# A graph attention layer on one core: loads of 2 MB with four held, the next group's lists earlier in a step, packings last and two tiles ahead

## What is computed

```python
h = relu(layernorm(x))
support = h @ weight                  # 4 heads of 64
f1, f2 = support . weight_u, support . weight_v
scores = leaky_relu(f1[m] + f2[n], 0.2) * adj[n, m]
attn   = softmax of scores over the m where scores != 0
out    = attn @ support + bias + h @ proj_w.T + proj_b
return x + out
```

## Time and profile before

| | |
|---|---|
| median of three runs | 863.06 us (859.76 to 864.25) |
| profiled execution | 860.12 us, of which the span 858.4 us |
| PE / DVE / POOL / ACT busy | 83% / 75% / 62% / 15% of the span |
| granted TensorE clock, mean | 0.889 of full speed |
| DMA | 63855 packets, 329.82 MB, mean 384 GB/s |
| DMA queues, share of 16 engines | q1 (SP) 83.8%, q0 (GpSimd's gathers) 11.1%, q10 (ScalarE's stores) 2.4% |
| loads of `adj` | 256 of 1 MB, 13.3 us from issue to landing (median) |
| gathers | 384, 6.2 us from issue to landing (median) |

### The profile page before, as it was taken

How to read it: one execution, slowest core, us unless ns; L and a number is a source line. 1 busy time by engine, 2 the same in 40 slices (tenths; PEclk the granted TensorE clock), 3 DMA queues, 4 the chain that set the end, 5 groups by cost and what they waited for, 6 DMA issues and landing times.

```text
span 858.4 us, 11157 instructions
## 1 busy us (share of the span) xinstructions
PE 710.9 (83%) x3011; PEld 434.2 (51%) x3011; DVE 643.1 (75%) x2740; ACT 129.3 (15%) x467; POOL 529.0 (62%) x598
## 2 busy tenths in 40 slices
PE   2989999999956878887888888788888878888865
PEld 0656666666513545454555445354544445454454
DVE  4556666657446988879869798977979787886887
ACT  0223333333210111000001011000011100000010
POOL 4344455454467776667766667676766766676570
PEclk9999999999966989888879898887989888988789
DMA  9999999999999999999999999999999999999971
GB/s 307 422 407 393 416 422 416 407 423 413 419 410 384 385 401 402 388 405 384 402 393 374 399 374 405 383 404 384 390 396 375 406 366 400 359 403 401 397 302 53
DMA packets 63855, 329.82 MB, mean 384 GB/s; under 512 B 12795, under 2 KB 15560, under 8 KB 31024
## 3 DMA queue, kind: packets, MB, share of 16 engines
q1 hardware_dynamic: 43056, 286.28, 83.8%
q0 software_dynamic: 18432, 34.30, 11.1%
q10 hardware_dynamic: 2304, 8.52, 2.4%
HBM read 328.99 MB, written 16.91 MB: 403 GB/s over the span
## 4 chain that ended last, share of the span: by engine, by line
PE 42%; DMA 25%; DVE 24%; issue 4%; POOL 3%; ACT 1%; POOLq 0%; ACTq 0%; SPq 0%
DMA adj_raw<-in_adj 21%; PE ps_words L400 11%; PE ps_agg L461 9%; PE ps_agg L381 7%; PE ps_two L381 6%; DVE att L933 5%; PE ps_two L400 5%; DVE cand L787 3%; DVE base L943 3%; POOL att L717 2%; DMA att<-support_table,idx 2%; PE ps_score L445 2%; DMA att<-in_x 1%; PE ps_words L392 1%; DMA support_table<-att 1%
## 5 line engine op out<-in xcount | busy, mean ns | idle before, releaser
L717 POOL DMA_INDIRECT att<-support_table,idx x384 | 417.4, 1087 | 188.7 <-issue 105.8
L400 PE MATMUL ps_words<-adj_raw,pack_w 128*128 128x512 fp8e4 x640 | 186.7, 428 | 25.4 <-DMA adj_raw<-in_adj 25.3
L461 PE MATMUL ps_agg<-att,ident 128*128 128x260 f32 x640 | 176.3, 428 | 8.5 <-DVE att L933 8.5
L461 PEld LDWEIGHTS ps_agg<-att,ident 128*128 128x128 f32 x640 | 135.1, 218 | 41.6 <-issue 18.6
L400 PE MATMUL ps_two<-adj_raw,pack_w 128*128 128x512 fp8e4 x384 | 118.9, 457 | 24.6 <-DMA adj_raw<-in_adj 24.5
L400 PEld LDWEIGHTS ps_words<-adj_raw,pack_w 128*128 128x128 bf16 x640 | 62.1, 106 | 125.3 <-DMA adj_raw<-in_adj 39.8
L787 DVE MAX8 cand<-ps_words 128x8 f32<-128x128 f32 x320 | 67.1, 281 | 66.3 <-PE ps_words L400 66.3
L933 DVE TENSOR_TENSOR att<-att 128x1536 f32<-128x1536 f32 x64 | 109.4, 1750 | 0.4 <-ACT att L625 0.4
L708 POOL COPY record<-att 128x8 f32<-128x8 f32 x64 | 13.4, 209 | 117.4 <-ACT att L569 117.4
L400 PEld LDWEIGHTS ps_two<-adj_raw,pack_w 128*128 128x128 bf16 x384 | 38.7, 113 | 91.5 <-DMA adj_raw<-in_adj 40.0
L381 PE MATMUL ps_agg<-w_all,hT 128*128 128x260 f32 x256 | 63.0, 389 | 4.1 <-ACT hT L565 4.1
(11 more groups left out here) (118 smaller groups left out, 821.2 us busy)
## 6 DMA issues: line engine op xcount, KB each, us to landing
adj_raw<-in_adj SPq DMA_DIRECT2D x256, 1024.0 KB, 13.3
support_table<-att ACTq DMA_DIRECT2D x16, 520.0 KB, 8.8
att<-in_x SPq DMA_DIRECT2D x16, 512.0 KB, 6.7
out<-base SPq DMA_DIRECT2D x15, 512.0 KB, 14.1
att<-support_table,idx POOLq DMA_INDIRECT x384, 6.2
out<-base SPq DMA_DIRECT2D x4, 128.0 KB, 1.9
w_all<-in_proj_wT SPq DMA_DIRECT2D x2, 128.0 KB, 6.0
w_all<-in_weight SPq DMA_DIRECT2D x2, 128.0 KB, 6.3
```

What stands on the lines that cost most here:

```text
L400: mm = nc.tensor.matmul(ps_words[buffer_of(t)][:, k * 512:(k + 1) * 512], pack_w[:, u * UT + s, :], adj_low[:, n % HELD, s, k * 512:(k + 1 ...
L461: mm = nc.tensor.matmul(ps_agg[:, b, 0:ROW], ident[:] if k < OWN else onehotT[:, g % RING, b], gathered[:, g % RING, b, k], start=(k == 0) ...
L717: pool.indirect_dma_start(gathered[:, g % RING, b, k, :], None, table, bass.IndirectOffsetOnAxis(idx[:, g % RING, b, k:k + 1], 0), bounds_ ...
```

## The change

Each tile comes in UNITS = 2 loads of 2 MB (16 KB for each partition) into HELD = 4 buffers, 8 MB in place of 6. To make room, several small tensors lie in others now. TensorE packs two tiles ahead in place of one, and all packings of a step stand at its end. In the steps of `AHEAD` (g = 1 to 26) `list_own(g)` and `offsets(g)` are done in the step before, in its middle, and `distances(g)` ahead of ScalarE's `exponential`; `edge_records(g)` becomes the first thing of TensorE's step, and on VectorE `one_hot` comes ahead of the pick and `list_spill` ahead of `scores`.

```diff
-UNITS = 4
-HELD = 6
+UNITS = 2
+HELD = 4
...
+    AHEAD = [g for g in range(1, LATE) if FIRST + sum(counts[:g - 1]) >= groups[g][0] + GS]
...
-        spare = sb("spare", [P, 4, HF])
+        uv_tmp = base[:, TILES - 4:].rearrange("p (q c) d -> p q c d", q=2)
+        uv_row = base[:, TILES - 6:TILES - 4]
+        projb_row = base[:, TILES - 7]
...
+        hT = onehot[:].rearrange("p a b m -> p a (b m)")
...
-                    if q > 0:
-                        pack_unit(g + 1, q - 1)
+                    if q > 0 and q % (LOAD // UNITS) == 0:
+                        pack_unit(g + 1, q // (LOAD // UNITS) - 1)
...
             pe.wait_ge(s_staged, TILES)
+            pack_places(FIRST + 1)
+            for u in range(UNITS):
+                pack_unit(FIRST + 1, u)
             for g in range(LATE):
-                new = [t + 1 for t in picks[g]]
-                offsets(g)
-                pack_places(new[0])
-                for u in range(UNITS // 2):
-                    pack_unit(new[0], u)
+                if g not in AHEAD:
+                    offsets(g)
+                if g in AHEAD:
+                    edge_records(g)
                 if g >= 2:
                     aggregate(g - 2, 0)
-                edge_records(g)
+                if g not in AHEAD:
+                    edge_records(g)
                 if g > 0:
                     row_scores(g - 1)
-                for u in range(UNITS // 2, UNITS):
-                    pack_unit(new[0], u)
+                if g >= 2:
+                    aggregate(g - 2, 1)
                 if g > 0:
                     edge_refs(g - 1)
-                if g >= 2:
-                    aggregate(g - 2, 1)
-                for t in new[1:]:
-                    pack_places(t)
-                    for u in range(UNITS):
-                        pack_unit(t, u)
+                if g + 1 in AHEAD:
+                    offsets(g + 1)
+                for t in picks[g]:
+                    if t + 2 < TILES - 1:
+                        pack_places(t + 2)
+                        for u in range(UNITS):
+                            pack_unit(t + 2, u)
...
-                if g > 0:
+                if g > 0 and g + 1 not in AHEAD:
                     exponential(g - 1)
                 if g + 1 >= RING:
                     clear(g + 1)
                 distances(g + 1)
+                if g > 0 and g + 1 in AHEAD:
+                    exponential(g - 1)
...
             for g in range(LATE):
+                if g in AHEAD:
+                    one_hot(g)
                 n = pick_words(picks[g][0], 0)
...
-                one_hot(g)
+                if g in AHEAD:
+                    list_spill(g)
+                else:
+                    one_hot(g)
                 if g > 0:
                     scores(g - 1)
-                list_spill(g)
+                if g not in AHEAD:
+                    list_spill(g)
+                if g + 1 in AHEAD:
+                    list_own(g + 1)
...
                 picked = split_words(picks[g][0], len(picks[g]), n)
-                list_own(g + 1)
+                if g + 1 not in AHEAD:
+                    list_own(g + 1)
```

More of the change, by code:

```diff
@@ L107, in gat_kernel @@
         assert 2 * XN + SN <= WIDE
-        uv_tmp = spare[:].rearrange("p (q c) d -> p q c d", q=2)
+        uv_tmp = base[:, TILES - 4:].rearrange("p (q c) d -> p q c d", q=2)
+        uv_row = base[:, TILES - 6:TILES - 4]
+        projb_row = base[:, TILES - 7]
+        place_hi = base[0:2, TILES - 9:TILES - 7].rearrange("p a d -> p (a d)").bitcast(BF16)
         ident = sb("ident", [P, P])
@@ L115, in gat_kernel @@
         w_all = sb("w_all", [P, KC, 2, ROW])
-        uv_row = sb("uv_row", [P, 2, HF])
         bias_row = sb("bias_row", [P, HF])
-        projb_row = sb("projb_row", [P, HF])
         eps_col = sb("eps_col", [P, 1])
@@ L122, in gat_kernel @@
         place = sb("place", [2, WORDS], BF16)
-        place_hi = sb("place_hi", [2, WORDS], BF16)
         bit_mask = sb("bit_mask", [P, BITS], I32)
@@ L131, in gat_kernel @@
         row_no = sb("row_no", [P, P])
-        hT = sb("hT", [P, 2, KC * P])
         stats = sb("stats", [P, LOAD, 6])
@@ L276, in gat_kernel @@
             att[:, P + q * H * P:P + (q + 1) * H * P].rearrange("p (h m) -> p h m", h=H) for q in range(5))
-        dn_out, dn_x, dn_xhat, dn_base = (spare[:, q, :] for q in range(4))
+        dn_out, dn_x, dn_xhat, dn_base = (base[:, q, :] for q in range(4))
         dn_rest = att[:, P + 5 * H * P:]
@@ L323, in _ @@
                              (bias_row[:, :], bias),
-                             (projb_row[:, :], proj_b.rearrange("(o d) -> o d", o=1))):
+                             (projb_row, proj_b.rearrange("(o d) -> o d", o=1))):
                 sp.dma_start(dst, src.to_broadcast([P, HF])).then_inc(s_w_in, 16)
@@ L697, in _ @@
             pool.wait_ge(s_w_in, 16 * W_LOADS)
-            const(pool.tensor_tensor(bias_row[:], bias_row[:], projb_row[:], ALU.add))
+            const(pool.tensor_tensor(bias_row[:], bias_row[:], projb_row, ALU.add))
             assert const.n == POOL_CONSTS
```

## The result

The changed kernel takes 872.12 us (median of six runs, 864.75 to 881.41), the kernel before 861.44 us beside it (six runs, 859.20 to 864.25): 1.0109 times as long, with a 95% interval of 1.0084 to 1.0133. A second comparison (e13) gave 1.0131 (1.0085 to 1.0177). It is slower, as forecast, by 1.1% where 2.5% was forecast. The profiled execution took 870.12 us, span 868.4.

A forecast was written before the change was run, and what follows sets the result against it. The prediction took the stream of adjacency loads as the bound, losing 3.2% to late buffers. Profiled 860.1 + 16.8 (pairs) + 4 (start) + 1 (end) = 882 us, scaled to a median of 885 us; range 845 to 902, likeliest case alone 866 to 903.

The forecast's parts named there:

- It loses 3.2% because buffers are given back late: From 300 to 780 us: the load stream bounds the kernel, but runs at 391 instead of 404 GB/s for late buffers.
- the gain of 16.8 us: Larger pool, packings two tiles ahead: a pair of steps falls from 37.7 to 36.5 us at best, over 14 pairs.
- the rival of 846 us: Load stream stays full in the second stretch: pair at 36.5 us, kernel faster at a median of 846 us; chance 0.28.
- Long rows starve the gathers: Second stretch: gathers wait a 16 KB row per packet, loads run dry; pair 38.9 us, +16.8 us; forecast's chance 0.57.
- dry stretches at 2.5 to 3.5 us a pair: Second stretch: 5 to 7 us net without loads, once in two pairs, giving 39 to 40 us a pair.
- a group of 12: Gathers of one step, issued every 1.30 us and served every 2.2: 3.7 are left behind it.
- the first rival: Stream stays full, among other reasons because earlier lists leave gathers enough time: 846 us; chance 0.28.
- The start, +4, between 0 and 17: Start of the second stretch: slower gathers make the scores of group 1 late, taken as +4 us.
- The end, +1, between 0 and 3: Last three steps: no gather shortage, but VectorE reaches the last two picks up to 3 us later; +1 us.
- The stream stays full: Second stretch: gathers do not hold up loads, pair at 36.5 us, median 846 us; chance 0.28.
- Edge records behind two packings: Both steps of a pair: TensorE's edge records wait behind packings that wait for loads; 40.4 us a pair, 901 us; chance 0.04.
- The gain is spent on the gathers: Second stretch: same queueing with shorter dry stretches, pair stays 37.7 us, 859 to 867 us; chance 0.11.

The follow-up runs named there:

- e13: The changed kernel once more, unaltered, against the kernel before: 875.85 us, ratio 1.0131.
- e4: The kernel before with eight 1 MB load buffers held instead of six, old step order: 861.06 us, ratio 0.9993 to the kernel before.
- e3: The kernel before's step order with 2 MB loads in 16 KB rows, four buffers: 930.79 us, ratio 1.0776 to the kernel before.
- e5: As e3, but each partition's 16 KB as two 8 KB rows: 876.51 us, ratio 1.000, where the kernel before takes 875 to 877 us.
- e14: The changed kernel with TensorE's order of before from step 28 on: 873.22 us, ratio 1.0129 to the kernel before.
- e17: The changed kernel with 2 MB loads as two 8 KB rows and TensorE's old order from step 28 on: 861.38 us, ratio 0.9989 to the kernel before.
- e10: As e9, but TensorE's order of before from step 28 on: 861.27 us, ratio 1.0000 to the kernel before.
- e9: The changed kernel's step order with 1 MB loads in 8 KB rows, eight held: 869.13 us, ratio 1.0081 to the kernel before.
- e15: As e4, but in steps 28 and 29 TensorE packs last and two tiles ahead: 868.52 us, ratio 1.0075 to the kernel before.
- e6: The program of e10 where the kernel before takes 875 to 877 us: 934.43 us, ratio 1.0705 to the kernel before.
- e16: The program of e17 in a slower comparison: 935.11 us against 874.71 for the kernel before, ratio 1.069.

## Why the prediction was wrong in size

**"It loses 3.2% because buffers are given back late": wrong, and the first step to fail.** From it came the gain of 16.8 us and the rival of 846 us. e4 takes the supposed cause away and gains nothing (0.3% at most, by its interval). The row for it was on the table: in the earlier trace rows the DMA share of that stretch is 1.00. Engines that are hardly ever idle can't be waiting for buffers. A part of the fall is that gathers move fewer bytes in the same time: 27.41 of 187.10 MB of the two queues, 14.6%, in 15.8% of the time. That is worth about 1%; what makes the deepest slices (340 GB/s from 732 to 744 us, at a share of 0.93) was not settled. SP's long waits only say that it is ahead.

**Long rows starve the gathers: right in mechanism, too dear in size.** 144 packets per 2 MB, turns of one packet, late gathers landing after 13 to 21 us, slices of 216 to 333: all as described, and e3 against e5 shows that the row does it. The forecast had dry stretches at 2.5 to 3.5 us a pair, 2.4 in the value taken, 34 us for 14 pairs. Measured are 12 us for the whole kernel, its start and end included: (1.0129 - 0.9989) x 861, e14 against e17. Of these, 4.3 us stand already at the first weighing (274.58 against 270.26). From there to the weighing 27 steps on, 13.5 pairs, a pair took 37.75 us before (509.57 in all) and 38.11 after (514.41), where 38.9 was forecast. In e14 it took 38.33 (517.48), and in e10, with short rows and the new order, 38.09 (514.21).

The term was mis-sized in how often a stretch runs dry: four low slices in 12.7 pairs, once in three, each followed by a plateau of 405 to 420 GB/s. One step of the working points there. It counted 9 packets of a load on an engine, but priced a turn at 1/8 of the load's time, as if only the eight rows took turns. By the counts of the two queues the completions take turns too, and a gather was served every 1.9 us and not every 2.2. By the prediction's own terms a group of 12 then leaves 12 - 18.2 / 1.9 = 2.4 gathers behind it instead of 3.7, an estimate that no run tests by itself. And long packets are cheaper than the 1% at most that I gave them: the loads' queue moved 160.27 MB in 81.5% of 480 us, 410 GB/s, against 396 before (159.69 MB in 84.0%) and 399 in e17. In the profiled run of after loss and gain cancelled in the mean rate (390 against 391 GB/s); in e14's they did not (384).

**The order's cover.** With the old order long rows cost 7.8%, with the new one 1.4%. The early lists do give the gathers time, as the first rival had it, only not all they need.

**The start, +4, between 0 and 17: right in size, by another group.** Scores of group 0 reach TensorE at 269.64 us instead of 261.44 and those of group 1 at 284.42 instead of 277.62, 6.8 us later. It is group 0 that waits for its gathers, 9.17 us until 268.22; group 1 only follows. With short rows the first weighing is not late (267.18 in e10, 270.26 in e17, 269.11 before, 275.36 after).

**The end, +1, between 0 and 3: a cause missing.** I compared the places of instructions one by one, and didn't ask what happens where the stream stops and no later step gives time back. There are two causes with one seat: the gathers' lateness in the change itself (7.10 us at 777.60), and, with short rows, the packing two tiles ahead in front of `offsets(29)` and the loads that it waits for (e9, e10, e15): 0.8%, or 7 us, where 1 was forecast. The two don't add, since a step that is late anyway finds its load landed.

**Rivals.** "The stream stays full" falls with its premise. "Edge records behind two packings" had the right kind of fault, in-order work behind a packing that waits for its load, at another instruction and only in the last steps, where it costs 7 us and not 38. "The gain is spent on the gathers" was the nearest: it had a pair of 37.7 us, and after has 38.1 up to 780 us.

The sum, 882 us against a profiled 870, came as near as it did by errors against each other: a gain of 17 us that didn't exist, and a loss of 34 us over the pairs that is 12 in all, start and end included. Its upper bound was also added up wrongly: 40.5 us a pair with the other upper bounds, +17 and +3, gives some 922 us and not 903.

## What to carry to other kernels

Before a dip in bandwidth is put down to late buffers, look at the engines' share: at 1.00 a deeper pool bought nothing here. Where small indirect DMAs share the engines with a bulk stream, count the packets of the two queues in a short window: one to one means that a small one waits a bulk row at each turn, and then the row length of the bulk loads, not their size, sets how long it waits. Large loads can be had with short rows. And an order that lets work run further ahead has to be unwound in the last steps: what is queued behind the packings of the last loads came 12 us late here, and cost 7 to 9 us at the end.

## What the hardware showed that I had not expected

With equal loads in flight, rows of 16 KB cost 7.8% and twice as many of 8 KB nothing (e3, e5, the latter on the slower kind; with the new order 1.3% and nothing, e14 and e17). The two queues take turns packet for packet, 151 to 151 in 6 us, although a packet of the loads carries 14 KB in the mean there and one of the gathers 2 (2.15 and 0.32 MB). Between the dips the long rows moved 405 to 420 GB/s, where the short ones of before moved 400 to 404 and those of e17, in the new order, up to 411. And the kernel before differs by 1.6% between the two kinds of comparison and the same program in the new order by over 8% (e10 and e6: 861 and 934 us; e17 and e16: 861 and 935 us), for a reason that was not found.
